# Moving one small exponential to the end of ScalarE's iteration in a graph-attention kernel

## The reference

```python
h = (x @ W.T).reshape(n, H, D)                 # 8 heads of 32
h_src, h_dst = h[src], h[dst]                  # dst is sorted
alpha = einsum(h_src, a_src) + einsum(h_dst, a_dst)
alpha = alpha + sum(relu(edge_attr @ edge_W.T + edge_b) * h_dst)
alpha = where(alpha >= 0, alpha, 0.2 * alpha)
amax = segment_max(alpha, dst)
ex = exp(alpha - amax[dst])
denom = segment_sum(ex, dst)
out = segment_sum(h_src * (ex / max(denom[dst], 1e-10)), dst) + bias
```

## Time and profile before

| | before |
|---|---|
| median of three runs | 3911.73 us |
| profiled execution: time, span | 3919.49 us, 3917.7 us |
| TensorE's granted clock, mean | 0.955 |
| busy over the span: PE, DVE, ACT, POOL | 88%, 66%, 53%, 49% |
| POOL's indirect DMAs in the edge loop | 1760, 0.955 to 0.960 us each |

### The profile page before, as it was taken

One profiled execution on the slowest core, in us unless ns is written; L12 is line 12 of the kernel. 1 busy time (PEld: TensorE's weight loads), 2 busy tenths in 40 slices (PEclk: granted clock), 3 DMA queues, 4 the chain that ended last, 5 costly groups with the idle time before them and its releaser, 6 DMA issues.

```text
span 3917.7 us, 89013 instructions
## 1 busy us (share of the span) xinstructions
PE 3439.8 (88%) x22054; PEld 2336.6 (60%) x22055; DVE 2602.4 (66%) x6056; ACT 2067.2 (53%) x5593; POOL 1927.7 (49%) x2172
## 2 busy tenths in 40 slices
PE   3788899977999999999999999999999869619999
PEld 2436788763555555555555555555555558518888
DVE  4656755547888888888888888888888734301211
ACT  2322233325777666777666776767667635323332
POOL 3402000006777777777777777777777301251111
PEclk7889999998999999999999999999999989859999
DMA  4731011115666666666666666666666330021110
GB/s 149 219 134 51 22 30 32 35 40 134 153 153 154 153 153 152 157 157 154 155 155 158 157 158 154 160 155 160 159 159 159 89 127 29 27 60 35 37 37 26
DMA packets 352304, 449.29 MB, mean 115 GB/s; under 512 B 170970, under 2 KB 275163, under 8 KB 350456
## 3 DMA queue, kind: packets, MB, share of 16 engines
q0 software_dynamic: 95568, 267.78, 27.7%
q10 hardware_dynamic: 108050, 122.83, 10.1%
q1 hardware_dynamic: 148231, 53.53, 5.7%
HBM read 389.57 MB, written 55.13 MB: 114 GB/s over the span
## 4 chain that ended last, share of the span: by engine, by line
PE 49%; DMA 10%; DVE 10%; issue 9%; SPq 8%; ACTq 5%; ACT 5%; POOL 3%; DVEq 1%; POOLq 0%
PE bank L1104 7%; PE bank L1040 6%; PE bank L1192 5%; PE bank L1204 5%; PE bank L1152 4%; PE bank L1004 4%; PE bank L1013 4%; SPq L421 4%; DMA al<-h_tab,idx 3%; SPq L424 3%; DMA link<-links 2%; PE bank L1061 2%; ACT dist L771 2%; DVE prod L1469 2%; POOL al L515 2%
## 5 line engine op out<-in xcount | busy, mean ns | idle before, releaser
L515 POOL DMA_INDIRECT al<-h_tab,idx x976 | 931.7, 955 | 302.7 <-issue 290.6
L515 POOL DMA_INDIRECT gbuf<-h_tab,idx x784 | 752.4, 960 | 406.1 <-issue 393.3
L753 ACT ACTIVATE enc<-bank,eb 128x512 f32<-128x512 f32 x880 | 551.5, 677 | 238.4 <-issue 168.5
L1469 DVE SCALAR_TENSOR_TENSOR prod<-enc,adst,bank 128x512 f32<-128x512 f32 x880 | 629.9, 737 | 66.1 <-PE bank L1040 63.5
L1040 PE MATMUL bank<-oneh_t,hbt 125*128 125x512 bf16 x2640 | 651.4, 383 | 13.6 <-DVE oneh_t L1460 8.1
L1104 PE MATMUL bank<-msg,oneh 128*125 128x264 f32 x2352 | 594.7, 396 | 20.4 <-DVE r L1557 18.2
L771 ACT ACTIVATE dist<-iota_n,dtile 128x125 f32<-128x125 f32 x1760 | 551.4, 385 | 0.6
L1104 PEld LDWEIGHTS bank<-msg,oneh 128*125 128x125 f32 x2352 | 421.1, 189 | 95.9 <-issue 27.6
L1040 PEld LDWEIGHTS bank<-oneh_t,hbt 125*128 x2640 | 232.9, 98 | 323.0 <-issue 127.6
L1104 PE MATMUL bank<-al,oneh 128*125 128x264 f32 x1168 | 293.9, 393 | 9.4 <-DVE r L1557 8.8
L1061 PE MATMUL bank<-prod,hsel 128*32 128x128 f32 x7040 | 285.7, 280 | 14.2 <-DVE prod L1469 14.0
(11 more groups left out here) (254 smaller groups left out, 5342.7 us busy)
## 6 DMA issues: line engine op xcount, KB each, us to landing
dstb<-dst ACTq DMA_DIRECT2D x440, 125.0 KB
al<-pen_d SPq DMA_DIRECT2D x1760, 4.0 KB
att<-attrx ACTq DMA_DIRECT2D x880, 24.0 KB
al<-h_tab,idx POOLq DMA_INDIRECT x976
link<-links SPq DMA_DIRECT2D x880, 0.2 KB
gbuf<-h_tab,idx POOLq DMA_INDIRECT x784
attrx<-al ACTq DMA_DIRECT2D x8, 1176.0 KB, 12.3
hsplit<-hb POOLq DMA_DIRECT2D x25, 375.0 KB, 6.2
```

The costliest lines, as they stand in the source:

```text
L515: pool.indirect_dma_start(slot(n)[:, c, :], None, h_tab, bass.IndirectOffsetOnAxis(ap=idx[g % 2][:, k:k + 1], axis=0)).then_inc(gathered[n ...
L753: m = act.activation(enc[n % 2][:, k, :], bank[k][:, :], ACT.Relu, bias=eb[:, k:k + 1])
L1469: v.scalar_tensor_tensor(prod[q][:, k, :], enc[q][:, k, :], adst[:, k:k + 1], bank[2 + (2 * n + k) % NDH][:, :], ALU.add, ALU.mult).then_i ...
```

## The change

The two lines that place `g_fac` in ACT's iteration move from behind `e_relu` to the end of the iteration, behind `m_oneh`. The condition (k = 4g+12), the instruction, what it waits for and what it signals stay as they are. No other engine's code changes.

```diff
                 if k < ITEMS:
                     e_relu(k)
-                if (g := group_at(k, 12)) is not None:
-                    g_fac(g)
                 if (g := group_at(k, 5)) is not None:
                     g_x(g)
...
                 if 0 <= k - 8 < ITEMS:
                     m_dt(k - 8, s_dt[k % G], t_dt[k % G])
                 if 0 <= k - 10 < ITEMS:
                     m_oneh(k - 10)
+                if (g := group_at(k, 12)) is not None:
+                    g_fac(g)
```

## The result

| | before | changed |
|---|---|---|
| median of six runs each | 3907.2 us | 3939.0 us |
| profiled execution: time, span | 3919.49, 3917.7 us | 3944.93, 3943.0 us |
| POOL, first gather that waited to last gather | 2137.0 us | 2165.5 us |
| last gather's start to the end of the last message sum | 47.1 us | 51.6 us |

The ratio is 1.0073 with a 95% interval of 1.0055 to 1.0090. Forecast were 3913.6 us and no change. The case that came true is the rival that had 0.06: the factor is late in every group.

The account below looks back on a forecast made before the run. POOL's gather queue was taken to bound the kernel. Steady part 0, start +1.9 and end 0 us gave +1.9 us on the median of 3911.73, so 3913.6 us, range 3898 to 3932 us.

Parts of the forecast that it names:

- the rival that had 0.06: At PE's wait for the factor, iterations 4g+13: factor late in every group, 80 us more, 3992 us; chance 0.06.
- What bounds the kernel before: Edge loop: POOL's gather queue sets the pace, 20.17 us a group of four items, not PE despite 95% busy.
- The cushion of 0.95 us: Per group in the loop: time the compute engines have to spare against POOL's 20.17 us.
- the free pace of 19.22 us: Compute's time for a group of four items, read from iteration 12 on, before SP's masks first came late.
- The signs that the prediction set for itself: Right if mid-loop gathers wait at most 0.3 us, 1.26 us apart, and DVE's L1484 wait stays about 1.6 us a group.
- The factor's place on ACT: Within ACT's iteration: the moved g_fac starts 4.8 us behind the relu's start and ends at about 5.0 us.
- PE would be late by 0.2 us, DVE not: Mid-loop, head of the next iteration: PE stalls about 0.2 us for the factor, DVE does not wait.
- ACT is given 2.4 us a group to catch up: Mid-loop on ACT: the hole before g_fac goes and DMA issue hides, saving up to 2.4 us a group.
- Repaid by the 0.4 us: Mid-loop on PE: its wait for the next iteration's relu goes, repaying the stall of about 0.2 us.
- The start: First g_fac delays iteration 13's message sum and POOL's gather after it: +1.9 us, bounds 1.4 and 2.7 us.
- The end: After the last gather: the last moved g_fac is still 0.5 us ahead of its reader; 0 us, within 1 us.
- The rival's price: Late factor in every group: stall of 1.7 us less 0.95, over 107 groups, 80 us.

Follow-up runs that it names:

- x_before_oneh: Changed kernel with g_fac one step earlier, between m_dt and m_oneh; 3909.5 us, ratio 0.9998 to the kernel before.
- y_dose2: Kernel before with e_enc's two PE matmuls done three times instead of once in one item of four; 3908.6 us, ratio 1.0003.
- y_dose5: Kernel before with e_enc's two PE matmuls done six times instead of once in one item of four; 3923.8 us, ratio 1.0039.
- x_load_last: Changed kernel with load_item and next_tile put behind g_fac in the iterations that have a g_fac; 3915.8 us, ratio 1.0014.

## Why the prediction was wrong, step by step

**What bounds the kernel before: right.** Less PE work (0.9994) and a freed ACT (x_before_oneh, 0.9998) change nothing, more PE work up to 0.43 us a group neither, and 1.08 us takes it to the edge. The cushion of 0.95 us from the two paces was right in size, and so was the free pace of 19.22 us: the changed kernel's group less its stall is 20.41 - 1.21 = 19.20 us. One word was not: by 1039 us compute was no longer quite free, DVE had waited 0.87 us for the masks at 1030 us. The signs that the prediction set for itself failed with the step below: the wait at L1484 is gone and gathers wait up to 2.7 us in mid-loop.

**The factor's place on ACT: right.** 4.8 us behind the relu was forecast for its start; 5.01 us on average (4.9 in the median) was measured.

**"PE would be late by 0.2 us, DVE not": wrong, and this is the step that failed.** DVE waits for the factor in 103 groups, 1.76 us on average; which of the two waits costs more was not separated. For PE, measured is 1.10 us more for the iteration, 1.21 over its undisturbed 4.89. The stall is what comes out when factor and PE are subtracted, and I read PE's side from one iteration. There PE's next L1061 stood 4.80 us behind the relu. It was a slack one: over 104 groups of the kernel before the relu is 0.56 us behind the first L1061 in the median (there 0.39), and PE needs 4.89 us to the next (there 5.19). With these and the same 5.0 us, the factor is late by 0.56 + 5.0 + 0.1 - 4.89 = 0.8 us before anything else happens, next to the edge of 0.95. The rest is the relu, which stands 0.83 us behind L1061 on average in the changed kernel (next paragraph), and 0.17 us more from relu to factor: 0.83 + 5.01 + 0.16 + 0.10 - 4.89 = 1.21.

**"ACT is given 2.4 us a group to catch up": wrong.** The relu did not come forward, it fell back, from 0.56 to 0.78 us behind L1061 (medians). In the iteration before, ACT waits for PE and DVE whatever it has saved, then does its one-hot and 1.75 us of register loads; the relu's place is set from there. What it had saved ended as waiting: in front of L753 ACT waits 91.6 us for DVE's products instead of 31.9, and in front of L760 it stands idle for 338.6 us instead of 266.5.

**"Repaid by the 0.4 us": right** (44.7 us to 1.4), and too small.

**The start: place right, size too small.** 1.9 us was forecast, 2.7 at most. In the changed kernel:

```profile
938.10 0.94 POOL L515 DMA_INDIRECT gbuf<-h_tab,idx  x1 [8.58 <-PE bank L1104]
...
940.61 0.16 ACT L795 ACTIVATE fac<-bank 125x8 f32<-125x8 f32 x1
...
940.87 1.08 PE L1061 MATMUL bank<-prod,hsel 128*32 128x128 f32 x16 [1.79 <-issue]
...
942.47 2.85 PE L1104 MATMUL bank<-msg,oneh 128*125 128x264 f32 x8
...
946.09 0.94 POOL L515 DMA_INDIRECT gbuf<-h_tab,idx  x1 [3.31 <-issue]
```

The two gathers are 7.99 us apart, 5.43 before, 2.6 us more. PE stalls 1.79 us as forecast, but then its L1061 lasts 1.08 us instead of 0.65 and its message sum 2.85 instead of 1.94: they run slower behind that pause.

**The end: wrong by 4.6 us.** I looked only at the last factors. Before, POOL's gather started 6.8 us (median over items) after the message sum that frees its slot; in the changed kernel 1.6 us. This lead of compute was a store that the end drew on. The other traces fit: with a lead of 6.3 us (y_dose2) the end takes 46.7 us, with 3.0 us (y_dose5) 51.6 us.

**The rival's price** of 80 us assumed a stall of 1.7 us in each group. It was 1.1 to 1.2, so the excess over the cushion was a third as large.

## What to carry to other kernels

When a result moves to the end of a queue, its lateness is a difference of two positions, and both want the median over all iterations, not one row; where it comes out near the cushion, say slower and price the excess. A cushion is an edge: up to it a stall is free, beyond it every group pays. Time saved on an engine that others hold in step does not move its next result forward.

## What the runs showed of the hardware

A pause of PE in one place of each group went with a lower clock where more idle time in shorter pauses did not. With two bf16 parts, from 1500 to 2000 us, PE is busy 438.1 us in the kernel before at a granted clock of 0.99, with 61 us of waits in 97 places; in the changed kernel it is busy 447.5 us at 0.94, with 50.1 us of waits in 25 places in front of L1061, 2.0 us each. In the changed kernel with all three parts that wait is 1.13 us and the clock stays at 0.99 to 1.00. By the levels of 2.4 and 1.2 GHz a mean of 0.94 is the lower one for about an eighth of the stretch.

Register loads on ACT can hide behind ACTIVATEs that are still running: the load between L760 and L764 leaves 0.78 us of idle time in the changed kernel's timeline, where ACT stood idle in front of L760 as well, and none in x_load_last, where L760 follows the relu directly. From 980 to 3080 us ACT's idle time in front of L764 is 84.9 us there and 1.0 us here.
